# Output projection of a gated cross-attention block: seven block products over all heads instead of one product per pair of heads

## What is computed

```python
x = x + jnp.tanh(g_xattn[0]) * _L0_xattn_ref(_layernorm(x, axis=-1), ctx_4096, mask_BxSxS2_bk0, ...)
x = x + jnp.tanh(g_ffn[0]) * _L0_ffn_ref(_layernorm(x, axis=-1), ...)
# in _L0_xattn_ref
h_q = (x @ w_q.T).reshape(b, lq, H, DH)
...
attn = jnp.einsum('bhqk,bkhd->bqhd', score, h_v).reshape(b, lq, H * DH)
out = attn @ w_out.T
```

## Time and profile before

| | us |
|---|---|
| median of 3 runs | 846.37 |
| lowest and highest | 845.33, 847.17 |
| the profiled execution | 845.15 |
| its span | 843.3 |
| TensorE busy | 832.3 (99%) |
| VectorE busy | 544.4 (65%) |
| ScalarE busy | 454.4 (54%) |
| GpSimd busy | 122.0 (14%) |

### The profile page before, as it was taken

One profiled execution on the slowest core, in us unless ns is written; L12 is line 12 of the kernel. 1 busy time (PEld: TensorE's weight loads), 2 busy tenths in 40 slices (PEclk: granted clock), 3 DMA queues, 4 the chain that ended last, 5 costly groups with the idle time before them and its releaser, 6 DMA issues.

```text
span 843.3 us, 12455 instructions
## 1 busy us (share of the span) xinstructions
PE 832.3 (99%) x4382; PEld 708.3 (84%) x4382; DVE 544.4 (65%) x926; ACT 454.4 (54%) x1097; POOL 122.0 (14%) x118
## 2 busy tenths in 40 slices
PE   7999999999999999999999999999999999999998
PEld 6787887888888888888888888888888888888886
DVE  5876477567777677767776777677762354434446
ACT  5446655447666666666666666666764643320001
POOL 1213230001111111111111111111110000002210
PEclk9999999999999999999999999999999999999999
DMA  8365356641432343334333433442546755630001
GB/s 305 120 192 173 121 170 173 221 157 51 132 117 96 126 132 116 97 125 133 113 100 126 132 96 117 126 131 82 182 158 210 259 193 194 204 124 1 1 26 75
DMA packets 76349, 113.94 MB, mean 135 GB/s; under 512 B 5760, under 2 KB 41216, under 8 KB 75776
## 3 DMA queue, kind: packets, MB, share of 16 engines
q1 hardware_dynamic: 76288, 113.16, 42.0%
HBM read 77.48 MB, written 35.65 MB: 134 GB/s over the span
## 4 chain that ended last, share of the span: by engine, by line
PE 93%; DVE 2%; DMA 2%; issue 1%; SPq 1%; ACT 1%; DVEq 0%; ACTq 0%
PE bank L282 76%; PE bank L1235 7%; PE bank L1218 6%; PE bank L1226 3%; DMA raw_v<-in_w_v 1%; DMA raw_wo<-in_w_o 1%; PE bank L1161 0%; PE bank L1306 0%; DVE stage L835 0%; DVE wv L774 0%; DVE stats L778 0%; DVE sv L808 0%; SPq L310 0%; DVE sv L802 0%; DVE cb L774 0%
## 5 line engine op out<-in xcount | busy, mean ns | idle before, releaser
L282 PE MATMUL bank<-wo_hl,at_hl 128*128 128x512 f32 x768 | 177.8, 391 | 0.0
L282 PE MATMUL bank<-xb,wq 128*128 128x512 f32 x672 | 177.3, 399 | 0.0
L282 PE MATMUL bank<-cb,wq 128*128 128x512 f32 x672 | 177.2, 399 | 0.0
L282 PEld LDWEIGHTS bank<-wo_hl,at_hl 128*128 128x128 f32 x768 | 143.2, 188 | 29.3
L282 PE MATMUL bank<-wv,cb 128*128 128x512 f32 x672 | 155.8, 393 | 5.3 <-DVE stage L835 4.2
L282 PEld LDWEIGHTS bank<-wv,cb 128*128 128x128 f32 x672 | 126.7, 189 | 33.3 <-DVE wv L774 6.1
L282 PEld LDWEIGHTS bank<-cb,wq 128*128 128x128 f32 x672 | 121.8, 188 | 23.0
L282 PEld LDWEIGHTS bank<-xb,wq 128*128 128x128 f32 x672 | 121.7, 188 | 23.0 <-issue 0.2
L506 POOL TENSOR_TENSOR bm<-bias_sb,mneg 128x512 f32<-128x512 f32 x64 | 74.6, 1165 | 427.9 <-DVE pr L928 392.1
L667 ACT ACTIVATE pr<-pr,nmax 128x128 f32<-128x128 f32 x256 | 99.2, 394 | 7.8 <-DVE nmax L930 7.8
L774 DVE TENSOR_TENSOR at_hl<-raw_at,at_hl 128x1024 fp32r<-128x1024 f32 x32 | 39.2, 1225 | 73.7 <-ACT wo_hl L683 73.5
(11 more groups left out here) (141 smaller groups left out, 943.5 us busy)
## 6 DMA issues: line engine op xcount, KB each, us to landing
v_spill<-stage SPq DMA_DIRECT2D x64, 256.0 KB, 3.1
raw<-in_w_qk SPq DMA_DIRECT2D x32, 512.0 KB, 5.4
v_sb<-v_spill SPq DMA_DIRECT2D x64, 256.0 KB, 3.2
...
```

Source lines behind the costliest of these rows:

```text
L282: mm = pe.matmul(dst, a, b, start=first and n == 0, stop=last and n == total - 1, skip_group_check=True)
```

## The change

The projection is computed transposed, out^T = w_out · attn^T, as a 2 x 2 block product in the dimensions output column (two of 256), token (two of 512) and head. The head dimension is split inside a "duo" of two pairs, so each duo gives a block product of its own, and each of M1 to M7 is accumulated over all 8 duos before the next product begins (`OORD`). That is 7 x 8 = 56 units; a unit is 12 matmuls of 128x512 from one pair of operands of 512 KB (`t_hl`) and 256 KB (`s_hl`). The finished products are put together in SBUF (`ct`) by `o_copy` on ScalarE and `o_sum` on VectorE, and TensorE transposes them back (`out_transposes`) ahead of `add_output`. Batches 4 to 7 are complete after five products, apart from the transposes, and come first (`ORDER`); 0 to 3 need the last.

The operands are sums. Those of the attention are made by VectorE during the attention steps (`t_sums`, 64 of 128x512) in four places that ScalarE copies into, and stored in DRAM (`t_spill`). Those of the weights are made in pieces (`s_sums`, 4 of 128x128 every second step), also stored (`s_spill`); the three unsummed weight blocks are copied there by 24 DMAs from DRAM to DRAM at the start of attention. To make room the ring of v goes from 5 to 2. In the first microseconds `v_sums` of the second product is put ahead of two weight sums and two GpSimd sums wait for VectorE's low parts. The last store goes in two halves.

```diff
-VRING = 5
+VRING = 2
...
+DUOS = PAIRS // 2
+UNITS = NP * DUOS
 ORING = 4
...
+S_AT = {M6: 0, M7: 1, M3: 2, M5: 3, M1: 4, M2: 5, M4: 6}
...
+EARLY_SPLITS = {(PAIRS - 2, 1): (0,), (PAIRS - 2, 2): (1,), (PAIRS - 2, 3): (2, 3), (PAIRS - 1, 0): (4,), (PAIRS - 1, 1): (5, 6),
+                (PAIRS - 1, 2): (7, 8), (PAIRS - 1, 3): (9, 10)}
+EARLY_LOADS = {(PAIRS - 2, 0): (0, 1), (PAIRS - 2, 1): (2, 3), (PAIRS - 2, 2): (4,), (PAIRS - 2, 3): (5,), (PAIRS - 1, 0): (6, 7),
+               (PAIRS - 1, 1): (8,), (PAIRS - 1, 2): (9, 10), (PAIRS - 1, 3): (11, 12)}
+FIRST_SPLIT = 11
+FIRST_LOAD = 13
...
-            def load_o(q):
-                for h in range(2):
-                    if q:
-                        sp.wait_ge(o_lo_ok, 4 * (q - 1) + 2 * h + 2)
-                    sp.dma_start(raw_at[:, h, :], at_dram[q, :, h, :, :].rearrange("p t n -> p (t n)")).then_inc(o_in[h], 16)
-                    sp.dma_start(raw_wo[:, h, :], w_o[q, :, D * h:D * h + D]).then_inc(o_in[h], 16)
+            for u in range(DUOS):
+                for m, k, i in ((M1, 0, 0), (M2, 1, 0), (M4, 1, 1)):
+                    sp.dma_start(s_dram[S_AT[m], u, :, :, :], wo_of(2 * u + k, i)).then_inc(a_copied, 16)
...
+            def store_at(s):
+                u, i = divmod(s, 8)
+                h, n = HT[s % 4]
...
+            def store_sums(s):
+                for u in (s // 8 - 1, s // 8):
+                    for k, h, step in T_SUMS:
+                        if 0 <= u < DUOS and 8 * u + step == s:
+                            sp.wait_ge(t_ok, t_count(u, k, h))
+                            if k in (1, 2):
+                                sp.dma_start(t_dram[T_AT[M5 if k == 1 else M6], u, :, h, :], x_at[:, h, :]).then_inc(x_stored[h], 16)
...
+                    sp.wait_ge(o_lo_ok, 2 * (n - ORING) + 1)
+                if m in (M1, M5, M6):
+                    for h in range(2):
+                        sp.wait_ge(x_stored[h], 16 * (3 * u + {M1: 1, M5: 2, M6: 3}[m]))
...
+                sp.dma_start(t_raw[n % ORING][:, :, :], t_dram[i, u, :, :, :]).then_inc(t_in[n % ORING], 16)
+                if n >= ORING:
+                    sp.wait_ge(o_lo_ok, 2 * (n - ORING) + 2)
...
+                sp.dma_start(s_raw[n % ORING][:, :, :], s_dram[S_AT[m], u, :, :, :]).then_inc(s_in[n % ORING], 16)
...
                 if p + 2 < PAIRS:
...
-                    h, n = HT[j]
-                    sp.wait_ge(at_ok, s + 1)
-                    sp.dma_start(at_dram[p, :, h, n, :], at_sb[:, s % 2, :]).then_inc(at_stored[s % 2], 16)
+                    store_at(s)
                     if s + VRING < STEPS:
                         sp.wait_ge(a_ps, s + 1)
                         load_v(s + VRING)
+                    store_sums(s)
+                    if s % 2 == 0:
...
-            for n in range(2):
-                sp.wait_ge(at_stored[n], 16 * STEPS // 2)
-            load_o(4)
-            sp.dma_start(acc[:, :, :], x).then_inc(x2_in, 16)
-            load_o(5)
...
+            for s in range(STEPS, STEPS + 3):
+                store_sums(s)
+            for h in range(2):
+                sp.wait_ge(x_stored[h], 16 * 3 * DUOS)
+                sp.wait_ge(y_stored[h], 16 * DUOS)
+            sp.wait_ge(z_stored, 16 * 2 * DUOS)
+            sp.wait_ge(g_stored[0], 16 * 3 * DUOS)
+            sp.wait_ge(g_stored[1], 16 * DUOS)
+            for n in range(FIRST_LOAD, UNITS):
+                load_o(n)
+                if n == FIRST_LOAD + 1:
+                    for own, at in ((slice(0, HALF), HALF), (slice(HALF, B), 0)):
+                        sp.dma_start(acc[:, own, :], x[:, at:at + HALF, :]).then_inc(x2_in, 16)
+                if n == FIRST_LOAD + 4:
...
+            def o_hi(n):
+                if n < ORING:
+                    act.wait_ge(prod, 2 * (NP * (PAIRS - 1) + (2, 2, 5, 5)[n]))
+                else:
+                    act.wait_ge(o_unit, n - ORING + 1)
+                act.wait_ge(t_in[n % ORING], 16 * (n // ORING) + 16)
+                act.activation(t_hl[n % ORING][:, 0, :, :], t_raw[n % ORING][:, :, :], ACT.Copy).then_inc(o_hi_ok, 1)
+                act.wait_ge(s_in[n % ORING], 16 * (n // ORING) + 16)
+                act.activation(s_hl[n % ORING][:, 0, :, :], s_raw[n % ORING][:, :, :], ACT.Copy).then_inc(o_hi_ok, 1)
...
-                    if s >= 2:
-                        act.wait_ge(at_stored[s % 2], 16 * (s // 2))
-                    act.activation(at_sb[:, s % 2, :], ps_at[:, :], ACT.Copy).then_inc(at_ok, 1)
...
+                    if i == 7:
+                        act.wait_ge(g_stored[0], 16 * (3 * u + 1))
+                        act.wait_ge(t_ok, t_count(u, 3, 1))
+                    act.activation(at_place(s), ps_at[:, :], ACT.Copy).then_inc(at_ok, 1)
...
+            def o_copy(i):
+                m = OORD[i]
+                act.wait_ge(o_unit, DUOS * (i + 1))
+                if i == 0:
...
+                for k in range(2):
+                    act.activation(ct[:, rows + k, W * half:W * half + W], (ps_oe if m == M5 else ps_oa)[k][:, :],
+                                   ACT.Copy).then_inc(oa_ok, 1)
+            act.wait_ge(gs_ok, 1)
+            for n in range(FIRST_SPLIT, UNITS):
+                o_hi(n)
+                if n == DUOS + 3:
+                    o_copy(0)
+                if n == FIRST_SPLIT + 4:
+                    act.wait_ge(x2_in, 32)
+                    for t in range(B):
+                        act.activation(acc[:, t, :], acc[:, t, :], ACT.Identity, bias=gated[:, 1, ORDER[t]:ORDER[t] + 1],
+                                       scale=gated[:, 0, ORDER[t]:ORDER[t] + 1]).then_inc(acc_ok, 1)
...
+                if k == 1:
+                    ve.wait_ge(at_ok, 8 * u + (3 if h == 0 else 4))
+                    ve.wait_ge(x_stored[h], 16 * (3 * u + 1))
+                    op = ve.tensor_tensor(x_at[:, h, :], y_at[:, h, :], x_at[:, h, :], ALU.subtract)
+                if k == 2:
...
+                    for k, h, step in T_SUMS:
+                        if 0 <= u < DUOS and 8 * u + step == s:
+                            t_sum(u, k, h)
+            def s_sums(r):
+                a11, a21, a12, a22 = s_piece[:, 0, 0, :], s_piece[:, 0, 1, :], s_piece[:, 1, 0, :], s_piece[:, 1, 1, :]
+                ve.wait_ge(piece_in, 32 * r + 32)
+                ve.tensor_tensor(a22, a21, a22, ALU.add).then_inc(piece_ok, 1)
+                ve.tensor_tensor(a21, a11, a21, ALU.subtract).then_inc(piece_ok, 1)
+                ve.wait_ge(piece_ok, 4 * r + 2)
+                ve.tensor_tensor(a11, a22, a11, ALU.subtract).then_inc(piece_ok, 1)
+                ve.wait_ge(piece_ok, 4 * r + 3)
+                ve.tensor_tensor(a12, a12, a11, ALU.subtract).then_inc(piece_ok, 1)
...
+            def output(n):
+                i, u = divmod(n, DUOS)
+                m = OORD[i]
...
+                pe.wait_ge(o_lo_ok, 2 * n + 2)
+                wo, at = s_hl[n % ORING], t_hl[n % ORING]
+                for h in range(2):
+                    for k in range(2):
+                        mm = three_passes(pe, banks[k][:, :], [((wo[:, 0, h, cols(k)], wo[:, 1, h, cols(k)]),
+                                                                (at[:, 0, h, :], at[:, 1, h, :]))],
+                                          first=m in (M1, M5, M2) and u == 0 and h == 0)
+                mm.then_inc(o_unit, 1)
...
+            def out_transposes(t):
+                pe.wait_ge(od_ok, 4 if t < HALF else 6)
+                if t in (0, 1, 2):
+                    pe.wait_ge((ea_ok, scored, at_ok)[t], (evac(PAIRS - 1, M4, 1), STEPS, STEPS)[t])
+                if t == 3:
+                    pe.wait_ge(od_ok, 6)
+                if t >= HALF:
+                    pe.wait_ge(oa_ok, 8)
+                if t in (6, 7):
...
-            for b in (0, 1):
-                for q in range(PAIRS - LAST_PAIRS, PAIRS - 1):
-                    output(q, b)
-            for b in (0, 1):
-                output(PAIRS - 1, b).then_inc(o_ps, 1)
-            last_outputs(2)
+            for n in range(DUOS, 5 * DUOS + 2):
+                output(n)
+            out_transposes(0)
+            out_transposes(1)
+            for n in range(42, 45):
+                output(n)
             x1_transposes(0)
             x1_transposes(1)
-            last_outputs(3)
+            output(45)
             lora(0)
-            last_outputs(4)
+            for n in range(46, 49):
+                output(n)
+            hw_transposes(0)
+            out_transposes(2)
+            out_transposes(3)
+            output(49)
             base(0)
+            output(50)
             base(1)
+            up(0)
             x1_transposes(2)
             x1_transposes(3)
-            last_outputs(5)
-            hw_transposes(0)
+            output(51)
             lora(1)
-            up(0)
-            last_outputs(6)
+            for n in range(52, 56):
+                output(n)
+            hw_transposes(1)
             base(2)
```

(10 more changed lines are left out.)

443 lines of the change are left out of this document (275 added, 168 removed).

## The result

The changed kernel takes 888.41 us (median of 4 runs, 886.39 to 890.9) against 845.85 for the kernel before: a ratio of 1.050, 95% interval 1.047 to 1.054. The forecast was 861.5, range 842 to 878. Slower was right; the size was too small by 27 us, and the time is 10 us outside the range.

The account below looks back on a forecast made before the run. TensorE was taken as the bound (busy 832.3 of 843.3 us). Terms -18.9 - 1.5 + 3 + 1 + 18 + 11.5 + 2.8 = +15.9 on 845.15 us, plus half a microsecond, gave 861.5; range 842 to 878.

Parts of the forecast that it names:

- Matmuls, 18.9 us less: Output projection on TensorE: 96 matmuls fewer, 32 transposes and a split last store added, net -18.9 us.
- so I keep the price: Output projection: operands keep their shape, so each matmul still takes 0.227 us; 96 fewer give -21.8 us.
- Start, 1.5: First microseconds: the first evacuation ahead of a weights' sum shortens TensorE's idle 3.77 us; 1.5 us gained, between 0 and 3.8.
- Attention, 3 and 1 for the copies: Attention: VectorE's new sums cost 3 us (0 to 10), the 24 DRAM-to-DRAM copies 1 us (0 to 9).
- work in the queue: Attention: 3.7 us of slack covers at most 1.7 to 2.9 us of sums ahead of the next scores.
- VectorE becomes the bound: Attention, slower rival: VectorE, 91% busy, loses two more microseconds per duo; +16, 877.5 us; chance 0.18.
- The last pair, 0: Last pair of attention: no added time; attention was taken to end about 643.6 us.
- The hand-over, 18: Passage from attention to projection: TensorE waits for late loads and splits of units; 18 us, between 14 and 23.
- the residual: Hand-over: the residual's load and ScalarE's scaling of it make TensorE wait 5.4 us before unit 15 and 4.9 before 16.
- Units 42 to 55, 11.5: Forecast for units 44 to 55: VectorE's first-four-batch work between splits makes TensorE wait five times; 11.5 us, between 4 and 14.
- that rule: Attention: a two-SBUF-input VectorE operation and GpSimd's SBUF reads block each other; 32 us more if every mask met a sum.
- After the last unit, 2.8: Ending: four batches remain instead of two, so TensorE waits more for VectorE's chain; +2.8 us, between 1 and 5.

Follow-up runs that it names:

- order55: The changed kernel with ScalarE's and VectorE's work on the first four batches put earlier among their splits; 864.3 us, 1.023.
- combo6: The changed kernel with batch work, loads and last-pair splits earlier, residual later, DRAM-to-DRAM copies dropped, GpSimd's bias additions held back; 841.4 us, 0.9950.
- piece_first: The changed kernel with the load of the next quarter of output weights first instead of last in SyncE's queue in odd attention steps; 881.2 us, 1.042.
- thin: The changed kernel with every sum VectorE makes for the products during attention cut to one column; 878.7 us, 1.039.
- late: The changed kernel with the residual's load moved from after unit 14's to after unit 22's, its scaling from split 15 to 28; 881.0 us, 1.041.
- fill2: The changed kernel with extra unread transposes keeping TensorE busy while it waits, run once more for a readable trace; 875.5 us.

## Why the prediction was wrong

**Matmuls, 18.9 us less: the count was right, "so I keep the price" was not.** Where the waits are gone (units 42 to 55 in order55 and combo6) a matmul takes 0.227 us, and the column "at full pace" adds up to the old span less 18.9 within about a microsecond. But the new kernel does not keep that price: the mean of its 672 matmuls rose from 391 to 415 ns with the clock, so the check that I gave (TensorE busy 19 us less) failed, since slow matmuls count as busy. What that cost is told under the stretches below.

**Start, 1.5: 1.1** in the profiled run. The changed kernels reach the first attention product between 194.6 and 197.9 us, so it drowns in variation; it was not tried alone.

**Attention, 3 and 1 for the copies: 8.3.** The copies cost 1.9, the sums nothing in thirteen pairs and about 1 in the fifteenth (29.4 in piece_first, 28.3 in thin). The step that failed is "work in the queue": I asked whether VectorE has time for its new operations, and costed only these. But each first sum of a quarter waits for a load, and this wait stands ahead of the scores. The rival "VectorE becomes the bound" falls with piece_first, though thin alone would have confirmed it.

**The last pair, 0: 5.2** (between 3.9 and 8.5 in the runs that changed nothing before or in it). I let attention end at 643.6 and thus took the splits in it as on time, a term put at nothing without a reason. The loop of load, split, copy, store and load that I walked from there on was already turning; loads ahead of stores mended the units behind it, earlier splits moved part of the wait.

**The hand-over, 18: 22.0.** The mechanism was right and so was the residual (waits of 3.86 and 2.59 for my 5.4 and 4.9, in late 0.65 and 2.14 further on); waits before units 9 and 11 were 3.34 and 4.47 for my 2.6 and 6.2. The waits alone are 14.9 us, fewer than forecast; slow units make up most of the rest, though without them (fill2) it would be only 1.7 less.

**Units 42 to 55, 11.5: 25.6.** Half of the whole miss. The five waits are the five that I named, 12.8 us together against 11.5. One was too small, the first: 3.22 for 1.6, which is GpSimd's additions beside the splits. I had weighed that rule for attention, where it changed nothing, and not here, where the earlier trace rows show GpSimd just ahead of the splits. Missing altogether is the clock, 9.5 to 11.6 us (fill2): the waits of 1.60 to 3.70 us here are followed by slow work, and the low-rank products run in it, on which the next wait depends.

**After the last unit, 2.8: 2.5** of idle time.

In short, some 13 us of the 28 missed (span against sum) are TensorE's clock, 5 the last pair, 4 waits of VectorE for loads, and the rest sizes of waits. The range had no term for the clock, so its upper end could not hold. What stays open: which waits lower the clock, since length alone does not decide it; what decides whether VectorE or GpSimd is held; and why the last pair takes anything from 26.2 to 30.8 us where nothing in it was changed.
